# An attention and feed-forward kernel: GpSimd makes the low parts of the absorbed weights' rotary columns, and VectorE rotates the second head before the other low parts

## The reference

```python
x = x + layernorm(mla_attention(layernorm(x)))       # 32 heads, causal
x = x + layernorm(qlora_ffn(layernorm(x)))

q = rmsnorm(h @ Wq_a, q_a_ln_w) @ Wq_b               # rank 192 -> 32 heads x (128 plain + 64 rotary)
ckv = h @ Wkv_a                                      # 64 compressed + 64 rotary, shared by all heads
kv = rmsnorm(ckv[..., :64], kv_a_ln_w) @ Wkv_b       # -> 32 heads x (128 keys + 128 values)
q_pe, k_pe = apply_rope(q_pe), apply_rope(k_pe)
scores = (qf @ kf^T) * (128 + 64) ** -0.5, causal mask, softmax
o = (probs @ v) @ Wo
```

## Time and profile before

| | us |
|---|---|
| median of 3 runs | 636.53 (635.88 to 636.82) |
| the profiled execution's own time | 634.38 |
| its span (first to last instruction) | 632.6 |
| TensorE busy | 577.4 (91%) |
| VectorE busy | 471.1 (74%) |
| ScalarE busy | 397.6 (63%) |
| GpSimd busy | 200.7 (32%) |
| mean granted TensorE clock | 0.989 of full |

### The profile page before, as it was taken

One profiled execution on the slowest core, in us unless ns is written; L12 is line 12 of the kernel. 1 busy time (PEld: TensorE's weight loads), 2 busy tenths in 40 slices (PEclk: granted clock), 3 DMA queues, 4 the chain that ended last, 5 costly groups with the idle time before them and its releaser, 6 DMA issues. The chain is left out here.

```text
span 632.6 us, 10775 instructions
## 1 busy us (share of the span) xinstructions
PE 577.4 (91%) x3336; PEld 430.0 (68%) x3336; DVE 471.1 (74%) x1235; ACT 397.6 (63%) x1157; POOL 200.7 (32%) x172
## 2 busy tenths in 40 slices
PE   5788999999999999999999999999979999979996
PEld 4676767767667676776777666767648888854564
DVE  5886787687777867778768777787867888878466
ACT  4555667767677676776776767767754454364343
POOL 3143434434443434433443444434100000024630
PEclk9898999999999999999999999999999999999998
DMA  8100222212212123121221232203556000001003
GB/s 315 31 1 30 73 67 73 97 47 79 90 67 72 47 90 100 47 73 63 75 99 47 77 85 75 71 18 115 175 184 266 2 1 1 0 31 50 1 13 122
DMA packets 19561, 46.93 MB, mean 74 GB/s; under 512 B 2608, under 2 KB 3120, under 8 KB 19248
## 3 DMA queue, kind: packets, MB, share of 16 engines
q1 hardware_dynamic: 19504, 46.23, 22.0%
HBM read 39.80 MB, written 6.42 MB: 73 GB/s over the span
## 5 line engine op out<-in xcount | busy, mean ns | idle before, releaser
L678 DVE CUSTOM_DVE_ANT_0 ss<-bank,cst 128x128 f32<-128x128 f32 (+3 forms) x256 | 124.0, 489 | 88.0 <-PE bank L1020 68.6
L416 ACT ACTIVATE pt<-bank 128x128 f32<-128x128 f32 (+3 forms) x256 | 110.7, 432 | 88.8 <-PE bank L1061 88.5
L408 ACT ACTIVATE pr<-ss,small 128x128 f32<-128x128 f32 (+3 forms) x256 | 142.5, 557 | 22.0 <-DVE small L678 21.8
L1018 PE MATMUL bank<-kt_hi,qt_hi 128*128 128x128 f32 (+3 forms) x256 | 101.2, 395 | 24.8 <-DVE small L678 22.1
L334 POOL TENSOR_TENSOR qt_lo<-qrot,qt_hi 128x512 fp32r<-128x512 f32 x64 | 83.9, 1310 | 118.4 <-ACT qt_hi L398 118.4
L327 POOL TENSOR_TENSOR qrot<-qrot,qswp 64x512 f32<-64x512 f32 x64 | 81.8, 1279 | 120.7 <-DVE qrot L670 119.2
L1061 PE MATMUL bank<-ident,pr 128*128 128x128 f32 x640 | 116.7, 280 | 0.6 <-ACT pr L408 0.6
L1061 PEld LDWEIGHTS bank<-ident,pr 128*128 128x128 f32 x640 | 75.7, 141 | 41.8 <-issue 18.5
L1019 PE MATMUL bank<-kt_lo,qt_hi 128*128 128x128 f32 (+3 forms) x256 | 83.4, 326 | 0.0
L1020 PE MATMUL bank<-kt_hi,qt_lo 128*128 128x128 f32 (+3 forms) x256 | 83.2, 325 | 0.0
L1073 PE MATMUL bank<-pt,kvn 128*64 128x256 f32 (+3 forms) x512 | 82.0, 442 | 0.7 <-ACT pt L416 0.7
(11 more groups left out here) (163 smaller groups left out, 1079.5 us busy)
## 6 DMA issues: line engine op xcount, KB each, us to landing
sv<-sv SPq DMA_DIRECT2D x16, 576.0 KB, 4.5
rsb<-rinv_scratch SPq DMA_DIRECT2D x64, 128.0 KB, 2.9
sq<-sq SPq DMA_DIRECT2D x16, 448.0 KB, 3.2
wvo_scratch<-vs SPq DMA_DIRECT2D x16, 256.0 KB, 2.0
wv_raw<-wvo_scratch SPq DMA_DIRECT2D x8, 512.0 KB, 4.4
xa<-x SPq DMA_DIRECT2D x8, 256.0 KB, 5.2
x<-x SPq DMA_DIRECT2D x1, 2048.0 KB, 10.2
out<-yo SPq DMA_DIRECT2D x8, 256.0 KB, 2.0
```

The lines of the kernel that those rows point to most:

```text
L408: nc.scalar.activation(pr[:, k % 4, 0:n], ss[:, RING[k], 0:n], ACT.Exp, bias=negmax[:, k % 8:k % 8 + 1], scale=-1.0, accum_out=rsum[:, k:k ...
L416: nc.scalar.activation(pt[:, b, h, 0:i + 1, i * P:(i + 1) * P], bank[2 + k % 2][:, 0:(i + 1) * P].rearrange("p (j q) -> p j q", q=P), ACT. ...
L678: nc.vector.tensor_tensor_reduce(out=ss[:, RING[k], 0:n], in0=bank[k % 2][:, 0:n], in1=mask[:, SEQ - n:SEQ], scale=-SCALE, scalar=3.4e38, ...
L1018: nc.tensor.matmul(out, w_hi, x_hi, start=start, stop=False)
```

## The change

VectorE's `weights_lo` keeps only the two subtractions of the absorbed columns. The two of the rotary columns go to GpSimd, in a new function `rope_lo`. ScalarE makes the two high parts of the rotary columns first and raises a new semaphore `rope_hi_made` after them. GpSimd waits for it, makes the low part of `w1`, waits for its own instruction, makes that of `w2`, and waits for that too (`rope_split`). It does so in `body(p)` of all pairs but the last, between `add_rotated` and `query_lo` of the first head of the second sequence (in the first pair: of the second head), and once in the prologue at t = 5. TensorE's first query of a pair and SP's `load_sq` wait for `rope_split` as well as for `wq_split`. On VectorE the call of `weights_lo` moves behind `rotate_own` of the second head in the same step.

```diff
+    rope = lambda k: sq[:, SQ_COLS - 4 * ROPE:SQ_COLS].rearrange("p (k h n) -> p k h n", k=2, h=2)[:, k]
@@ SP
             def load_sq(p):
                 sp.wait_ge(a.wq_split, p)
+                sp.wait_ge(a.rope_split, p)
@@ GpSimd
+            def rope_lo(w):
+                pool.wait_ge(a.rope_hi_made, w + 1)
+                nc.gpsimd.tensor_tensor(w1_lo[:, :, RKV:P], rope(0), w1_hi[:, :, RKV:P].bitcast(F32), ALU.subtract)\
+                  .then_inc(a.rope_lo_made, 1)
+                pool.wait_ge(a.rope_lo_made, w + 1)
+                nc.gpsimd.tensor_tensor(w2[64:P, :, RKV:P], rope(1)[64:P], w2[64:P, :, RKV:P].bitcast(F32), ALU.subtract)\
+                  .then_inc(a.rope_split, 1)
+                pool.wait_ge(a.rope_split, w + 1)
+
-            def body(p, last=False):
+            def body(p, first=False, last=False):
                 for b in (1,) if last else (1, 0):
                     for h in range(2):
                         gi = 4 * p + (2 if b else 4) + h
                         pool.wait_ge(a.qt_split, gi)
                         add_rotated(gi, h)
+                        if b and h == first and not last:
+                            pool.wait_ge(a.pe_added, gi + 1)
+                            rope_lo(p + 1)
                         query_lo(gi, b, h, gi + 1)
...
+                if t == 5:
+                    rope_lo(0)
@@ ScalarE, weights_hi
-                nc.scalar.activation(w1_hi[:, :, 0:RKV], pv[:, 0], ACT.Copy)
-                nc.scalar.activation(w1_hi[:, :, RKV:P], rv[:, 0], ACT.Copy)
-                nc.scalar.activation(w2[:, :, 0:RKV], pv[:, 1], ACT.Copy)
-                nc.scalar.activation(w2[:, :, RKV:P], rv[:, 1], ACT.Copy).then_inc(a.wq_hi_made, 1)
+                nc.scalar.activation(w1_hi[:, :, RKV:P], rope(0), ACT.Copy)
+                nc.scalar.activation(w2[:, :, RKV:P], rope(1), ACT.Copy).then_inc(a.rope_hi_made, 1)
+                nc.scalar.activation(w1_hi[:, :, 0:RKV], pv[:, 0], ACT.Copy)
+                nc.scalar.activation(w2[:, :, 0:RKV], pv[:, 1], ACT.Copy).then_inc(a.wq_hi_made, 1)
@@ VectorE, weights_lo
-                for cols, src in ((slice(0, RKV), pv), (slice(RKV, P), rv)):
-                    nc.vector.tensor_tensor(w1_lo[:, :, cols], src[:, 0], w1_hi[:, :, cols].bitcast(F32), ALU.subtract)
-                    last = nc.vector.tensor_tensor(w2[64:P, :, cols], src[64:P, 1], w2[64:P, :, cols].bitcast(F32),
-                                                   ALU.subtract)
-                last.then_inc(a.wq_split, 1)
+                nc.vector.tensor_tensor(w1_lo[:, :, 0:RKV], pv[:, 0], w1_hi[:, :, 0:RKV].bitcast(F32), ALU.subtract)
+                nc.vector.tensor_tensor(w2[64:P, :, 0:RKV], pv[64:P, 1], w2[64:P, :, 0:RKV].bitcast(F32), ALU.subtract)\
+                  .then_inc(a.wq_split, 1)
@@ VectorE, body
-                    if k == (4 if first else 2) and not last:
-                        weights_lo(p + 1)
...
                         elif r in (0, 2) and not (first and k == 0):
                             rotate_own(gi + r // 2, r // 2)
+                        if k == (4 if first else 2) and not last:
+                            weights_lo(p + 1)
@@ TensorE, query
                 if w is not None:
                     pe.wait_ge(a.wq_split, w + 1)
+                    pe.wait_ge(a.rope_split, w + 1)
```

More of the change, by code:

```diff
@@ L208, in build @@
         q_scaled q_doubled qn_made krot_parts kvn_made qk_turned qk_hi_made qk_split""")
+    rope = lambda k: sq[:, SQ_COLS - 4 * ROPE:SQ_COLS].rearrange("p (k h n) -> p k h n", k=2, h=2)[:, k]
     x_in = [nc.alloc_semaphore(f"x_in{t}") for t in range(TB)]
-    a = sems("attention", """sq_in sv_in wq_made wq_hi_made wq_split q_made q_rotated pe_added qt_hi_made qt_split
+    a = sems("attention", """sq_in sv_in wq_made wq_hi_made wq_split rope_hi_made rope_lo_made rope_split q_made q_rotated pe_added qt_hi_made qt_split
         s_made s_masked exp_made p_turned p_moved o_made rinv_made r_made r_moved r_out r_in o_scaled
@@ L356, in _ @@
                     pool.wait_ge(a.qt_split, t - TB)
-            body(0)
+            body(0, first=True)
             for p in range(1, PAIRS - 1):
@@ L387, in weights_hi @@
                 pv = absorbed(w)[:, 0:4 * RKV].rearrange("p (k h n) -> p k h n", k=2, h=2)
-                rv = sq[:, SQ_COLS - 4 * ROPE:SQ_COLS].rearrange("p (k h n) -> p k h n", k=2, h=2)
+                nc.scalar.activation(w1_hi[:, :, RKV:P], rope(0), ACT.Copy)
+                nc.scalar.activation(w2[:, :, RKV:P], rope(1), ACT.Copy).then_inc(a.rope_hi_made, 1)
                 nc.scalar.activation(w1_hi[:, :, 0:RKV], pv[:, 0], ACT.Copy)
-                nc.scalar.activation(w1_hi[:, :, RKV:P], rv[:, 0], ACT.Copy)
-                nc.scalar.activation(w2[:, :, 0:RKV], pv[:, 1], ACT.Copy)
-                nc.scalar.activation(w2[:, :, RKV:P], rv[:, 1], ACT.Copy).then_inc(a.wq_hi_made, 1)
+                nc.scalar.activation(w2[:, :, 0:RKV], pv[:, 1], ACT.Copy).then_inc(a.wq_hi_made, 1)
             def query_hi(gi, b, h, s_done=None):
```

## The result

The changed kernel takes 609.35 us (median of 4 runs, 608.17 to 609.48), against 636.2 us for the kernel before (4 runs, 634.84 to 636.82): a ratio of 0.9577 with a 95% interval of 0.9557 to 0.9597. Forecast were 615.5 us and a range down to 612.8. In later comparisons the same kernel took 610.6 and 610.3 us beside 636.2 and 635.0.

A forecast was written before the change was run, and what follows sets the result against it. TensorE was taken as the bound, stalled 1.53 us in each of 14 pairs. The sum -21.4 + 0.75 (first pair) - 0.3 (prologue) = -21.0 us took the median of 636.5 to 615.5 us; range 612.8 to 620.5.

The forecast's parts named there:

- The place, the cause and the count: TensorE stalls before unit 7's scores in pairs 1 to 14, as GpSimd holds VectorE's two-SBUF-input low part; 1.5 us each.
- TensorE lacks 25.73 - 24.20 = 1.53 us per pair: Later pairs: pair length less TensorE's busy time taken as the stall, gained in full; 21.4 us over 14 pairs.
- more than 22.6 us cannot be gained: Whole kernel: upper bound on the gain from 14 x 1.53, the prologue's 0.6 and a little less first-pair loss.
- VectorE: Later pairs: the mask of unit 5 starts right behind its scores and ends at 236.95, with 0.6 us of slack.
- GpSimd's price: Each new 128-column subtraction on GpSimd takes 0.46 us, between ends of 0.32 and 0.91.
- GpSimd's chain: Later pairs: GpSimd's late addition makes ScalarE wait 0.80 us, absorbed before TensorE turns unit 7, with 0.55 us slack left.
- Rival A: GpSimd's chain through ScalarE to TensorE passes its slack; 4 to 15 us back, 619 to 631 us; chance 0.10.
- Rival B: GpSimd blocks VectorE even with a PSUM operand; 3 to 6 us lost, 618 to 621 us; chance 0.04.
- First pair: GpSimd's rotary low parts come behind its addition, so TensorE waits longer for the weights; 0.75 us lost.
- Rival C: GpSimd's instructions cost about 1.5 us or more each, making a longer TensorE stall; about 643 us, slower; chance 0.03.
- rival D: Another TensorE wait hidden under the stall appears and takes back half the gain; 626 us; chance 0.05.
- Prologue: VectorE sheds two subtractions, but GpSimd's may collide with its scaling; 0.6 gained to 0.4 lost, 0.3 us gained taken.

The follow-up runs named there:

- e1: The kernel before with only the order changed: VectorE's four low parts behind the second head's rotation, nothing to GpSimd; 626.8 us, ratio 0.9856.
- e3: e1 with VectorE making the two rotary low parts before the two from the bank, nothing to GpSimd; 614.0 us, ratio 0.9653.
- e2: The changed kernel with `weights_lo` called at its old place, ahead of the rotation; 612.1 us, ratio 0.9632.
- e6: The changed kernel with VectorE making the low part of w1's absorbed columns five times, four more than needed; 626.1 us, ratio 0.9851.
- e0: The changed kernel run again without edits, beside e1 to e3; 610.6 us, ratio 0.9602.
- f1: The changed kernel run once more without edits, beside f2 to f4; 610.3 us, ratio 0.9602.
- f4: The changed kernel with GpSimd making its first rotary subtraction two times more than needed, 1.07 us more work; 619.4 us.
- e4b: The changed kernel with GpSimd making its first rotary subtraction four times more than needed, 2.13 us more work; 635.3 us, ratio 0.9994.
- f3: The changed kernel with VectorE making all four low parts for pair 0 in the prologue, as before the change; 611.2 us.
- e5: The changed kernel with GpSimd making the first pair's rotary low parts one query earlier, at the first head; 608.5 us, ratio 0.957.
- f2: The kernel of e5 run again, beside f1; 608.4 us, ratio 0.9573.

## Why the prediction was wrong, point by point

- **The place, the cause and the count: right.** One stall in each of 14 later pairs, in front of unit 7's scores, made by a two-input instruction of VectorE that GpSimd holds. e1 to e3 show it: the order alone gains 0.60 us a pair, moving the two instructions to GpSimd alone 1.59 (e2), the order with the rotary ones first 1.58 (e3).
- **The term that failed: "TensorE lacks 25.73 - 24.20 = 1.53 us per pair", and "14 x 1.53 = 21.4 us".** The pair became shorter by 1.80 us, 14 x 1.80 = 25.2: the term was 3.8 us too small, and the bound of the range ("more than 22.6 us cannot be gained") rested on the same number. (636.5 - 22.6 is 613.9; that the range went on to 612.8 came from no term.) The recorded idle time leaves out the run-out of the matmul ahead, 0.27 us; e6 shows that this holds for another stall of another size, e2 that a stall of 0.19 us is not shown at all. Length minus busy time was therefore a lower bound, and I used it as an upper one. The trace before had the answer: the weight load behind the gap had idled for 1.83 us, and the starts 237.26 and 239.06 stand in the earlier trace rows. With the term put right, the gain would be 21.0 + 3.8 = 24.8 us; the later comparisons measured 25.6 (e0) and 24.7 (f1).
- **The rest of the first comparison: luck.** It measured 26.9 us, 2.1 more than these 24.8. The granted clock of its four runs of the changed kernel was 0.989 to 0.993, that of e0 and f1 0.984 to 0.994 with medians of 0.989, and within f1 the runs with the highest clocks are the shortest. That the clock made the whole of the 2.1 us is not shown.
- **VectorE: right, its slack too large.** The mask was forecast right behind the scores, with 0.6 us of slack against a recorded end; it has 0.37 against the true demand (e6).
- **GpSimd's price: right.** 0.46 us was taken between ends of 0.32 and 0.91; 459 and 456 ns were measured. A hand-off to itself takes 0.07 and not 0.14.
- **GpSimd's chain: right in kind and in slack.** Forecast were a wait of ScalarE of 0.80 us and a slack of 0.55; measured were 0.53 and 0.55 to 0.56. Two errors in it cancel. Counted from the turning of unit 4, TensorE asks for the exponent of unit 7 after 253.57 - 249.25 = 4.32 us (forecast 241.85 - 237.26 = 4.59), and ScalarE goes on after its wait at 2.05 (forecast 2.33). Rival A did not happen; f4 and e4b show what it would have cost.
- **Rival B: refuted.** VectorE's two subtractions from the bank take 0.29 beside GpSimd's. The Trainium skill's limit (SBUF — State Buffer, Who interferes with whom: two SBUF inputs on VectorE, and a read of SBUF on GpSimd) agrees with these rows: 295 ns at most from the bank, beside GpSimd too, and 1271 from `sq` before. The Trainium skill's general warning (Perfetto Trace Analysis, Optimizing Scalar/DVE Operations: offloading between the two might not help) did not come true here: moving the two gained 1.59 us a pair (e2).
- **First pair: right.** The wait is 3.0 us in the profile after (forecast 3.0, before 2.29).
- **Rival C and rival D: not met.** No instruction of GpSimd came near 1.5 us; e4b shows what it takes. Of D, the gain taken back elsewhere, 1.2 us are seen, in the feed-forward part (see the sum).
- **Prologue: 0.3 gained fits, and luck lies on top.** In the two profiled executions the first low part of the first pair comes 1.6 us earlier (56.51 and 54.88), but in f1, the same kernel as the second, at 56.32. The clock goes with most of the difference: up to 50 us it was at its lower level for about 6.8 us before, for 3.4 in the first trace of the changed kernel and for 6.8 in f1 (rows in the last section). At equal time on the lower level the change gains 0.2 (56.51 and 56.32) or 0.4 us (f3's 55.24 and 54.88); each of these is a difference of two single traces. The collision that the prediction feared in the prologue is there and small. VectorE's scaling takes 0.69 where it took 0.55, and the instruction behind it starts 0.61 instead of 0.46 us after it:

```profile
23.35 0.69 DVE L779 TENSOR_SCALAR xn<-xa,st 128x512 f32<-128x512 f32 x1
...
23.31 0.46 POOL L342 TENSOR_TENSOR w_lo<-sq,w_hi 128x128 fp32r<-128x128 f32 x1
23.84 0.52 POOL L345 TENSOR_TENSOR w<-sq,w 64x128 fp32r<-64x128 f32 x1
```

- **The sum.** For the profiled executions: 1.6 gained up to the first pair (most of it the clock's, as said), 0.4 lost in it (at the reciprocal of pair 1 the gain is 88.48 - 85.50 = 2.98, of which 1.80 belongs to a pair), 25.2 gained in 14 pairs: 26.4 at 397 us. The span is shorter by 25.2; the 1.2 between are lost in the feed-forward part, whose code is untouched, where TensorE now waits 1.6 us for one low part and waited 0.5 before. The medians of the three comparisons differ by 24.7 to 26.9, around the 25.2 of the pairs.

## What to carry to other kernels

What a stall of a pipelined engine costs is read from start to start: from the start ahead of the gap to the start behind it, less the same distance where there is no gap, never from idle time or from length minus busy time alone, which hid 0.23 to 0.27 us of each stall here and all of a short one. When one instruction takes four times what its twin takes, look for the instruction of another engine that ends with it; making the two instructions 0.6 us earlier on their own engine, with the order of e1 (e3), gained 22.1 us where moving them to another engine gained 25.6. Work put on an idle engine is free only up to the slack of the chain behind it, here 0.55 us on an engine that is idle for half of the time.

## What the runs showed of the hardware

- A subtraction on VectorE whose two inputs lie in SBUF takes 0.29 us, or lasts until 0.15 us after the end of the instruction that GpSimd runs (1.27 here: 237.95 against 237.80); with one input in PSUM it takes 0.29 beside GpSimd.
- A run of equal pairs with TensorE "busy" for 100% of the time can still lose 0.2 us in each (e2, 24.15 against 23.94).
- Between subtractions of GpSimd, each of which waits for the one before, lie 0.07 us; 128 columns take it 0.46 us on 128 partitions and on 64.
- The granted clock of the first 50 us differs between traces of the same kernel. It has two levels, full (2.4 GHz) and half of it (1.2 GHz; a short window shows it as 0.50, e0 from 61.93 to 62.00), so 10 us with a mean of 0.83 had about 3.4 us at the lower one. Windows from 20 to 50 us (last but two columns: clock, DMA share, GB/s), before:

```profile
20.00:30.00 10.00, 6.80 (x43) 6.07 (x42) 8.92 (x34) 5.01 (x23) 1.09 (x4) 0.91 0.16 48
30.00:40.00 10.00, 9.80 (x60) 9.08 (x59) 8.38 (x31) 5.24 (x24) 1.10 (x5) 0.92 0.00 1
40.00:50.00 10.00, 7.04 (x34) 5.81 (x33) 6.38 (x24) 5.97 (x19) 6.11 (x8) 0.83 0.00 0
```

and after, the first trace:

```profile
20.00:30.00 10.00, 6.71 (x47) 5.72 (x45) 8.95 (x33) 5.75 (x28) 1.98 (x6) 1.00 0.16 48
30.00:40.00 10.00, 9.61 (x59) 8.59 (x59) 8.98 (x33) 4.29 (x19) 2.41 (x7) 1.00 0.00 1
40.00:50.00 10.00, 7.20 (x35) 6.26 (x35) 6.70 (x23) 7.29 (x22) 4.82 (x6) 0.83 0.00 0
```

and f1, the same kernel, where the first two windows are at 1.00 too:

```profile
40.00:50.00 10.00, 7.31 (x27) 6.14 (x26) 5.68 (x20) 6.15 (x20) 5.10 (x6) 0.66 0.00 0
```

  The first low part of the first pair comes the later, the longer the lower level lasted before it: at 54.61 with none of it (e0), at 54.70 to 55.24 with 3.4 us in four traces (the first of the changed kernel, e2, f3, f4), and at 55.65 to 57.32 with 6.8 us in nine (the kernel before, e1, e3 and e4b among them; the 57.32 is e6, which does more work there). In 20 to 30 us the changed kernel had 1.00 in all three traces, but e5 and f2, which differ from it only later, had 0.84 and 0.83. TensorE idles and works in turns in this part of every kernel here, with over 3 us without a matmul in 20 to 30 us in both rows above; why the clock falls earlier or later was not settled.
